# Two-layer transformer block, head size 8: the head outputs of a step issued ahead of its scores

## The chip, the cores and the metric

The kernel runs on one core of one Trainium2 chip. The metric is the time of one execution on the device in microseconds (us). Engines are named as the profile does: PE is TensorE (PEld its weight loads), ACT ScalarE, DVE VectorE, POOL GpSimd, SP SyncE.

## The reference

Sixty-four sequences of 128 tokens with width 160 go through two transformer layers. Each layer is self-attention, cross-attention over 77 context tokens of width 96, and a gated feed-forward part, each with a layer norm ahead of it and a residual behind it. The first layer has 20 heads of size 8, the second 20 heads of size 64. The part that matters here is the first layer's pair of attentions:

```python
def _attn(x, ctx, wq, wk, wv, wo, bo, heads):      # heads = 20, dh = 8
    q = (x @ wq).reshape(b, n, heads, dh).transpose(0, 2, 1, 3)
    k = (ctx @ wk).reshape(b, j, heads, dh).transpose(0, 2, 1, 3)
    v = (ctx @ wv).reshape(b, j, heads, dh).transpose(0, 2, 1, 3)
    sim = jnp.einsum('bhid,bhjd->bhij', q, k) * scale
    a = jax.nn.softmax(sim, axis=-1)
    out = jnp.einsum('bhij,bhjd->bhid', a, v)
    return out.transpose(0, 2, 1, 3).reshape(b, n, heads * dh) @ wo + bo
h1 = _ln(x, n1_g, n1_b)
x = _attn(h1, h1, q1, k1, v1, o1_w, o1_b, heads) + x
h2 = _ln(x, n2_g, n2_b)
x = _attn(h2, context, q2, k2, v2, o2_w, o2_b, heads) + x
```

## The kernel before

`attention_small` computes both attentions with head size 8. It takes four sequences at a time (a quad), 16 quads of self-attention and then 16 of cross-attention; the texts call these two halves the first and the second layer of this stage. A quad has ten units of work: five groups of four heads, each in two halves of two heads. So there are 320 units, numbered n, and as many steps k; the steps of a quad are its places s = k % 10. All loops are unrolled, and every engine has a hand-written order of its own, with semaphores between them.

Each unit goes through these hands:
1. `scores_step` (PE, line 890): eight products of two heads and four sequences into `scores`. Each uses 31 rows of the array, in two of its four row groups.
2. DVE takes the negated maximum over the keys (line 817) into `negmax`. At even places PE transposes the maxima of a finished group (line 1013), ACT copies them to `shift` (line 754), and a DMA that POOL issues (line 686) writes them as one more row of `q_stack`, so that the transposed scores come out with the maximum already subtracted.
3. `scoresT_step` (PE, line 908), five steps behind (`ST_LAG`): the transposed scores with that row, 32 rows of the array each, into `scoresT`. When its unit is k - 5 and the scores' unit is k, the two use different row groups.
4. ACT takes the exponential of the whole unit at once (line 731) into one of two `probs` buffers.
5. `values_step` (PE, line 927), six steps behind (`PV_LAG`): the head outputs, 16 records with 32 columns of the array each, into the single bank `heads_bank`. After the second half of a group ACT copies the bank to `heads` (line 761).

Both `scoresT` (its place) and `probs` tie these together. The transposed scores of unit n wait for the exponential of n - 1, the head outputs of unit n for the exponential of n; since the first is five steps and the second six steps behind, both wait in one step for the same exponential:

```python
# scoresT_step(k - 5)
if due(n):
    pe.wait_ge(s_exp, n)
...
# values_step(k - 6)
pe.wait_ge(s_exp, n + 1)
if half == 0 and due(n // 2):
    pe.wait_ge(s_heads, 5 * (k // QUNITS) + g)
```

Besides, a step of PE has other work, called the extras here: the projections for the next quad (places 0 to 3, line 332), norm transposes (4 and 6, line 428), the values' projections (8 and 9), the spreading of the reciprocal sums (1 and 3, line 1029), the output products (5 and 7, line 1087), and in the second layer fillers without use for the result (`keep_busy`, line 874).

ACT's order within a step is: the copy of a projected tile (line 720, places 1 to 4), the exponential (731), a copy of projected values (741, places 9 and 0), the norm's scaling (440, places 5 and 7), a rounding copy (450, places 6 and 8), the shift (754, even places), the copy of the head outputs (761, odd places). The exponential waits for this step's transposed scores, the copy at the end for this step's head outputs.

Ahead of this stage stand loads and constants, behind it the feed-forward part of the first layer and the second layer with its wide heads; these stages are the rest of the span.

Of the kernel before, what the change touches and what calls it, by code (L numbers as in the profile page):

```python
# [41 lines left out]
def live(value, total):  # L42

    return not isinstance(value, int) or 0 <= value < total


def due(count):

    return not isinstance(count, int) or count > 0
# [432 lines left out]
def attention_small(m, tag, wo, context, params, weights, state, front, following, following_params, first_gelu):  # L482
# [8 lines left out]
    ST_LAG, PV_LAG = 5, 6  # L491
# [6 lines left out]
    with ExitStack() as ctx:  # L498
# [89 lines left out]
        def maxima_at(k):  # L588

            s, local = k % QUNITS, k // QUNITS  # L590
            if s % 2:
                return None
            local, g = (local, s // 2 - 1) if s else (local - 1, GROUPS - 1)
            return (g, local % 2, 5 * local + g, local) if live(local, TOTAL) else None
# [267 lines left out]
        def _(pe):  # L862
# [14 lines left out]
            def scores_step(k):  # L877

                n, s, par, g, half = unit_of(k), k % QUNITS, k // QUNITS % 2, k % QUNITS // 2, k % 2
                if not live(n, LAST_UNIT):  # L880
                    return
                NK, EVEN = keys_of(quad_of(k)), even_of(quad_of(k))
                if due(n):
                    pe.wait_ge(s_negmax, n)
                if s < 2:
                    pe.wait_ge(s_stack[half], 16 * STACK_DMAS * (quad_of(k) + 1))
                for a in range(QUAD):
                    for jj in range(2):
                        rows = slice(32 * (2 * half + jj), 32 * (2 * half + jj) + 31)
                        last = nc.tensor.matmul(scores[:, jj, a * EVEN:(a + 1) * EVEN], q_stack[par][rows, g, a * P:(a + 1) * P],  # L890
                                                k_stack[par][rows, g, a * NK:a * NK + EVEN], start=True, stop=True)
                last.then_inc(s_scores, 1)

            def scoresT_step(k):

                n, par, g, half = unit_of(k), k // QUNITS % 2, k % QUNITS // 2, k % 2
                if not live(n, LAST_UNIT):
                    return
                NK = keys_of(quad_of(k))
                if due(n):  # L900
                    pe.wait_ge(s_exp, n)
                if half == 0:
                    order = 5 * (k // QUNITS) + g
                    pe.wait_ge(s_shift_in[order % 2], 16 * (order // 2 + 1))
                for a in range(QUAD):
                    for jj in range(2):
                        rows = slice(32 * (2 * half + jj), 32 * (2 * half + jj) + 32)
                        last = nc.tensor.matmul(scoresT[0:NK, jj, a * P:(a + 1) * P], k_stack[par][rows, g, a * NK:(a + 1) * NK],  # L908
                                                q_stack[par][rows, g, a * P:(a + 1) * P], start=True, stop=True)
                last.then_inc(s_scoresT, 1)  # L910

            def values_step(k):

                n, par, g, half = unit_of(k), k // QUNITS % 2, k % QUNITS // 2, k % 2
                if not live(n, LAST_UNIT):
                    return
                NK = keys_of(quad_of(k))
# [3 lines that stand above are left out]
                if k % QUNITS == 0:  # L921
                    pe.wait_ge(s_v, 2 * (quad_of(k) + 1))
                for r in range(2):
                    for b in range(2):
                        for jj in range(2):
                            c, a, col = 2 * b + jj, 2 * r + b, (2 * half + r) * P
                            last = nc.tensor.matmul(heads_bank[32 * c:32 * c + 32, col:col + P],  # L927
                                                    v[par][0:NK, a, GROUP * g + 2 * half + jj, :],
                                                    probs[k % 2][0:NK, jj, a * P:(a + 1) * P], start=True, stop=True)
                last.then_inc(s_pv, 1)  # L930
# [61 lines left out]
            def waiting(place):  # L992


                for i in range(START):
                    nc.tensor.matmul(place[:], wparts[0][0][0][:, 0:P], norm.high[0][:], start=True, stop=True)

            def step(k):
                s, local, ahead = k % QUNITS, k // QUNITS, quad_of(k) + 2
                if k == 0:  # L1000
                    waiting(max_bank)
                scores_step(k)
                scoresT_step(k - ST_LAG)
                values_step(k - PV_LAG)
                made = maxima_at(k)
                if made:
                    g, par, order, n = made
# [90 lines left out]
            def prepare(k):  # L1098
                if k == QUNITS - 1:
                    weights[0].wait_split(pe)  # L1100

            run(pe, step, prepare)


# [1258 lines left out]
```

## Time and profile before

| what | us |
|---|---|
| median of three runs | 3530.03 (3522.09 to 3530.37) |
| the profiled execution's own time | 3525.25 |
| its span, first to last instruction | 3522.1 |
| PE busy | 3457.5 (98% of the span) |
| DVE busy | 2319.1 (66%) |
| ACT busy | 2104.8 (60%) |
| POOL busy | 1290.1 (37%) |

PE is the busy engine over the whole span. The stage with head size 8 begins its steps near 35 us and its last one ends near 868 us. The granted clock is the share of full speed at which PE was allowed to run; 1.00 is 2.4 GHz, 0.50 is 1.2 GHz. Its mean over the span is 0.996.

### The profile page before, as it was taken

The numbers are of one execution on the slowest core, as the hardware profiler recorded it, in microseconds if no ns is written. First come the engines' busy times: TensorE is split into PE (matmuls) and PEld (weight loads), VectorE is DVE, ScalarE is ACT, GpSimd is POOL, SyncE is SP. The second block draws the span as 40 slices with busy tenths as digits, with TensorE's granted clock in tenths as the row PEclk, the third lists the DMA queues.
The fourth block names the chain that finished last, engine by engine and source line by source line (L and its number), as shares of the span: only waits on it lengthen the run. The fifth ranks groups of instructions, "written<-read, shape, count | busy, mean of one in ns | idle before, by whom it ended". The sixth has DMA issues, their size and how long they took to land. (4 is left out here: it accounts for less than half of the span.)

```text
span 3522.1 us, 96791 instructions
## 1 busy us (share of the span) xinstructions
PE 3457.5 (98%) x39199; PEld 3077.1 (87%) x39199; DVE 2319.1 (66%) x3902; ACT 2104.8 (60%) x5278; POOL 1290.1 (37%) x1278
## 2 busy tenths in 40 slices
PE   8999999999999999999999999899999999999999
PEld 6777778787888899999999999889999999998888
DVE  5788866665455567676776676656666666667454
ACT  4777777776334666566566556566666666665343
POOL 5333333332343243333333333433333333334332
PEclk9999999999999999999999999999999999999999
DMA  4444433321100100000000000000000000000000
GB/s 105 114 107 109 98 87 84 89 76 54 46 0 0 37 2 2 2 1 1 2 1 2 1 2 2 23 7 5 3 5 3 5 3 5 3 3 1 20 22 23
DMA packets 99756, 101.68 MB, mean 29 GB/s; under 512 B 31249, under 2 KB 74129, under 8 KB 99345
## 3 DMA queue, kind: packets, MB, share of 16 engines
q1 hardware_dynamic: 93408, 94.41, 10.6%
q8 instruction: 301, 4.93, 0.6%
q0 software_dynamic: 5120, 1.35, 0.2%
q14 instruction: 111, 0.90, 0.1%
q10 hardware_dynamic: 816, 0.08, 0.0%
HBM read 20.76 MB, written 5.24 MB: 7 GB/s over the span
## 5 line engine op out<-in xcount | busy, mean ns | idle before, releaser
L1217 POOL TENSOR_TENSOR a_probs<-a_probs,a_rsums 128x1024 f32<-128x1024 f32 x160 | 303.5, 1897 | 710.8 <-DVE a_rsums L1346 708.7
L1249 ACT ACTIVATE a_probs<-a_scores_banks,a_negmax 128x128 f32<-128x128 f32 x1280 | 371.4, 386 | 197.5 <-DVE a_negmax L1325 197.5
L1666 POOL TENSOR_TENSOR c_probs<-c_probs,c_rsums 128x616 f32<-128x616 f32 x160 | 233.9, 1462 | 618.1 <-DVE c_rsums L1795 618.1
L731 ACT ACTIVATE s_probs<-s_scoresT_banks 128x1024 f32<-128x1024 f32 (+1 forms) x320 | 327.1, 1022 | 182.7 <-PE s_scoresT_banks L908 180.4
L817 DVE TENSOR_REDUCE s_negmax<-s_scores_banks 128x8 f32<-128x1024 f32 (+1 forms) x320 | 322.2, 1007 | 134.3 <-PE s_scores_banks L890 130.9
L1703 ACT ACTIVATE c_probs<-c_scores_banks,c_negmax 128x77 f32<-128x77 f32 x1280 | 311.6, 334 | 133.9 <-DVE c_negmax L1783 133.1
L1354 DVE COPY a_probsT<-a_scores_banks 128x1024 f32<-128x1024 f32 x160 | 195.6, 1223 | 170.0 <-PE a_scores_banks L1422 169.9
L1783 DVE TENSOR_REDUCE c_negmax<-c_scores_banks 128x4 f32<-128x308 f32 x320 | 138.2, 473 | 238.8 <-PE c_scores_banks L1874 195.3
L2169 DVE SCALAR_TENSOR_TENSOR f_hidden<-f_value_bank,bias,f_gate 128x512 f32<-128x512 f32 x160 | 120.1, 750 | 246.8 <-ACT f_gate L2144 244.8
L686 POOL DMA_DIRECT2D s_q_stack<-s_shift x160 | 93.6, 585 | 488.9 <-ACT s_shift L754 482.5
L2144 ACT ACTIVATE f_gate<-f_gate_bank,bias 128x512 f32<-128x512 f32 x160 | 109.9, 687 | 260.9 <-PE f_value_bank L332 260.8
L1325 DVE TENSOR_REDUCE a_negmax<-a_scores_banks 128x4 f32<-128x512 f32 x320 | 198.6, 683 | 53.2 <-PE a_scores_banks L1409 53.2
L890 PEld LDWEIGHTS s_scores_banks<-s_k_stack,s_q_stack 31*128 31x128 f32 x2560 | 166.7, 185 | 72.5 <-issue 39.8
L1344 DVE TENSOR_REDUCE a_sums<-a_probs 128x8 f32<-128x1024 f32 x160 | 194.2, 1214 | 52.1 <-ACT a_probs L1249 52.1
L890 PE MATMUL s_scores_banks<-s_k_stack,s_q_stack 31*128 31x128 f32 (+1 forms) x2560 | 208.0, 283 | 6.0 <-DVE s_negmax L817 3.2
L927 PE MATMUL s_heads_bank<-s_probs,s_v 128*32 128x128 f32 (+1 forms) x5120 | 206.6, 279 | 0.7
L1714 ACT COPY c_queries<-c_even_bank 128x512 f32<-128x512 f32 x160 | 93.7, 586 | 189.6 <-PE c_even_bank L332 187.5
L2227 PEld LDWEIGHTS f_y_bank<-f_w_out,f_hidden 128*128 128x128 f32 x1280 | 190.9, 189 | 17.1 <-DVE f_hidden L2169 3.9
L1939 PE MATMUL c_y_bank<-w_out,c_outT 128*128 128x160 f32 x1280 | 203.0, 302 | 0.9 <-DVE c_outT L1774 0.9
L2227 PE MATMUL f_y_bank<-f_w_out,f_hidden 128*128 128x160 f32 x1280 | 200.5, 299 | 2.5 <-DVE f_hidden L2169 2.5
L1459 PE MATMUL a_y_bank<-w_out,a_outT 128*128 128x160 f32 x1280 | 199.6, 303 | 1.8 <-DVE x_tokens L1336 1.8
L1271 ACT COPY a_v<-a_even_bank 128x512 f32<-128x512 f32 (+1 forms) x192 | 96.0, 519 | 168.6 <-PE a_even_bank L332 99.0
(319 smaller groups left out, 10473.8 us busy)
## 6 DMA issues: line engine op xcount, KB each, us to landing
s_q_stack<-front SPq DMA_DIRECT2D x192, 160.0 KB, 3.3
s_k_stack<-front SPq DMA_DIRECT2D x96, 160.0 KB, 3.8
s_out<-s_heads SPq DMA_DIRECT2D x128, 80.0 KB, 2.5
s_k_stack<-front SPq DMA_DIRECT2D x96, 96.2 KB, 3.0
x_tokens<-in_x SPq DMA_DIRECT2D x16, 320.0 KB, 3.7
out_x<-x_tokens SPq DMA_DIRECT2D x16, 320.0 KB, 2.4
s_q_stack<-s_shift POOLq DMA_DIRECT2D x160, 8.0 KB, 2.5
s_ctx_in<-in_ctx SPq DMA_DIRECT2D x16, 115.5 KB
```

The source lines that it names most:

```text
L731: nc.scalar.activation(probs[i][0:NK, :, :], scoresT[0:NK, :, :], ACT.Exp).then_inc(s_exp, 1)
L817: nc.vector.tensor_reduce(out=negmax[order % 2][:, half * 2 * QUAD:(half + 1) * 2 * QUAD].rearrange("p (j a) -> p j a", j=2), in_=scores[: ...
L890: last = nc.tensor.matmul(scores[:, jj, a * EVEN:(a + 1) * EVEN], q_stack[par][rows, g, a * P:(a + 1) * P], k_stack[par][rows, g, a * NK:a ...
L927: last = nc.tensor.matmul(heads_bank[32 * c:32 * c + 32, col:col + P], v[par][0:NK, a, GROUP * g + 2 * half + jj, :], probs[k % 2][0:NK, j ...
L1217: nc.gpsimd.tensor_tensor(probs[n % 4][:], probs[n % 4][:], rsums[n % 2][:].unsqueeze(2).broadcast_to([P, UNIT, TOK]), ALU.mult).then_inc( ...
L1249: last_one = nc.scalar.activation(probs[n % 4][:, h, :], scores[n % 2][:, h // GROUP, h % GROUP * TOK:(h % GROUP + 1) * TOK], ACT.Exp, bia ...
L1325: nc.vector.tensor_reduce(out=negmax[n % 2][:, j * GROUP:(j + 1) * GROUP], in_=scores[n % 2][:, j, :].rearrange("p (h k) -> p h k", h=GROU ...
L1459: last = nc.tensor.matmul(y_bank[:, a * D:(a + 1) * D], outT[n % 2][:, (2 * c + a) * P:(2 * c + a + 1) * P], m.wo[:, 2 * g + c, :], start= ...
L1666: nc.gpsimd.tensor_tensor(probs[n % 5][:], probs[n % 5][:], rsums[n % 2][:].unsqueeze(2).broadcast_to([P, UNIT, NK]), ALU.mult).then_inc(s ...
L1703: last_one = nc.scalar.activation(probs[n % 5][:, h, :], scores[:, h // GROUP, h % GROUP * NK:(h % GROUP + 1) * NK], ACT.Exp, bias=negmax[ ...
L1939: last = nc.tensor.matmul(y_bank[:, a * D:(a + 1) * D], outT[n % 2][:, (2 * c + a) * P:(2 * c + a + 1) * P], m.wo[:, 2 * g + c, :], start= ...
L2227: last = nc.tensor.matmul(y_bank[a // 2][:, a % 2 * D:(a % 2 + 1) * D], hidden[(k - 1) % 2][:, a * P:(a + 1) * P], w_out[:, t, :], start=( ...
```

## The change

In each step of PE, the head outputs of unit k - 6 are issued first, then the scores of unit k and the transposed scores of unit k - 5. No instruction is added or removed, the semaphores and lags are the same, and the orders of the other engines are not touched.

```diff
@@ -999,9 +999,9 @@
                 s, local, ahead = k % QUNITS, k // QUNITS, quad_of(k) + 2
                 if k == 0:
                     waiting(max_bank)
+                values_step(k - PV_LAG)
                 scores_step(k)
                 scoresT_step(k - ST_LAG)
-                values_step(k - PV_LAG)
                 made = maxima_at(k)
                 if made:
                     g, par, order, n = made
```

## Rows read from the trace of the kernel before

**Rows 1.** Busy us (x instructions), engines PE, PEld, DVE, ACT, POOL; clock, DMA, GB/s.

```profile
35.00:868.00 833.00, 820.25 (x13190) 640.28 (x13190) 598.32 (x941) 610.72 (x976) 289.79 (x361) 1.00 0.37 93
```

**Rows 2.** Waits, 35 to 868 us: waiter, awaited, total us, times, longest.

```profile
PEld s_scores_banks L890 <- DVE s_negmax L817: 28.4, 76, 1.0
...
PEld s_scoresT_banks L908 <- ACT s_probs L731: 0.8, 2, 0.4
```

**Rows 3.** Timeline of PE, place 0, first layer: start, duration, instruction.

```profile
319.69 0.33 PE L890 MATMUL s_scores_banks<-s_k_stack,s_q_stack 31*128 31x128 f32 x2
319.72 0.33 PE L908 MATMUL s_scoresT_banks<-s_q_stack,s_k_stack 32*128 32x128 f32 x2
...
320.40 0.65 PE L927 MATMUL s_heads_bank<-s_probs,s_v 128*32 128x128 f32 x16
320.98 0.28 PE L1013 MATMUL s_max_bank<-ident,s_negmax 128*16 128x128 f32 x1
```

**Rows 4.** Timeline of ACT, places 2 to 1 of the first layer.

```profile
301.08 1.03 ACT L731 ACTIVATE s_probs<-s_scoresT_banks 128x1024 f32<-128x1024 f32 x1 [0.98 <-PE s_scoresT_banks L908]
...
303.40 1.03 ACT L731 ACTIVATE s_probs<-s_scoresT_banks 128x1024 f32<-128x1024 f32 x1
...
306.54 1.02 ACT L731 ACTIVATE s_probs<-s_scoresT_banks 128x1024 f32<-128x1024 f32 x1 [0.98 <-PE s_scoresT_banks L908]
...
308.55 1.02 ACT L731 ACTIVATE s_probs<-s_scoresT_banks 128x1024 f32<-128x1024 f32 x1 [0.85 <-PE s_scoresT_banks L908]
...
310.13 0.59 ACT L761 COPY s_heads<-s_heads_bank 128x512 f32<-128x512 f32 x1
311.10 1.02 ACT L731 ACTIVATE s_probs<-s_scoresT_banks 128x1024 f32<-128x1024 f32 x1 [0.38 <-PE s_scoresT_banks L908]
...
318.17 1.02 ACT L731 ACTIVATE s_probs<-s_scoresT_banks 128x1024 f32<-128x1024 f32 x1 [0.84 <-PE s_scoresT_banks L908]
...
319.60 0.66 ACT L761 COPY s_heads<-s_heads_bank 128x512 f32<-128x512 f32 x1
320.49 1.02 ACT L731 ACTIVATE s_probs<-s_scoresT_banks 128x1024 f32<-128x1024 f32 x1 [0.23 <-PE s_scoresT_banks L908]
...
322.90 1.02 ACT L731 ACTIVATE s_probs<-s_scoresT_banks 128x1024 f32<-128x1024 f32 x1
```

**Rows 5.** Timeline of ACT, places 2 to 0 of the second layer.

```profile
503.85 1.02 ACT L731 ACTIVATE s_probs<-s_scoresT_banks 77x1024 f32<-77x1024 f32 x1 [0.96 <-PE s_scoresT_banks L908]
...
505.92 1.02 ACT L731 ACTIVATE s_probs<-s_scoresT_banks 77x1024 f32<-77x1024 f32 x1 [0.25 <-PE s_scoresT_banks L908]
506.84 0.57 ACT L761 COPY s_heads<-s_heads_bank 128x512 f32<-128x512 f32 x1
...
508.51 1.02 ACT L731 ACTIVATE s_probs<-s_scoresT_banks 77x1024 f32<-77x1024 f32 x1 [0.79 <-PE s_scoresT_banks L908]
...
510.61 1.02 ACT L731 ACTIVATE s_probs<-s_scoresT_banks 77x1024 f32<-77x1024 f32 x1 [0.94 <-PE s_scoresT_banks L908]
...
512.19 0.57 ACT L761 COPY s_heads<-s_heads_bank 128x512 f32<-128x512 f32 x1
513.48 1.02 ACT L731 ACTIVATE s_probs<-s_scoresT_banks 77x1024 f32<-77x1024 f32 x1 [0.71 <-PE s_scoresT_banks L908]
...
520.88 1.02 ACT L731 ACTIVATE s_probs<-s_scoresT_banks 77x1024 f32<-77x1024 f32 x1 [0.75 <-PE s_scoresT_banks L908]
...
523.73 1.02 ACT L731 ACTIVATE s_probs<-s_scoresT_banks 77x1024 f32<-77x1024 f32 x1 [0.25 <-PE s_scoresT_banks L908]
```

**Rows 6.** Timeline of PE near 127 us; in brackets idle time, releaser.

```profile
126.85 0.66 PE L908 MATMUL s_scoresT_banks<-s_q_stack,s_k_stack 32*128 32x128 f32 x8 [0.72 <-DMA s_q_stack<-s_shift]
127.44 0.43 PE L927 MATMUL s_heads_bank<-s_probs,s_v 128*32 128x128 f32 x8
```

**Rows 7.** Timeline of PE near 96 us; in brackets idle time, releaser.

```profile
96.35 0.37 PE L1013 MATMUL s_max_bank<-ident,s_negmax 128*16 128x128 f32 x1 [1.82 <-DVE s_out L804]
```

**Rows 8.** Busy times and granted clock as in rows 1, 96.09 to 102.92.

```profile
96.09:102.92 6.83, 6.57 (x45) 4.27 (x46) 4.33 (x7) 3.44 (x7) 3.57 (x4) 0.50 0.01 1
```

## The prediction

> **What bounds the kernel now.** I first looked at the busy times of the stretch in which the changed loop runs. TensorE is busy for 820.25 of 833 us there, ScalarE for 610.72, VectorE for 598.32 [rows 1]. So one step of this loop costs what TensorE's own instructions cost, and anything that makes TensorE stand still is added to the time. The wait rows say how little it stands now: for VectorE's maxima before the scores 28.4 us in all, and for ScalarE's exponentials 0.8 us in two places [rows 2]. The reader should not conclude that the exponentials are far from being needed. The timeline has to tell how much earlier than needed each one ends.
>
> One step of TensorE [rows 3]: scores and transposed scores start together at 319.69 and 319.72 (they lie in different row groups and run side by side), the head outputs follow at 320.40, the rest of the step ("the extras": maxima, projections, norm transposes, output products, fillers) at 320.98. The exponential starts at 320.49 [rows 4], 0.80 us after the pair began. So it runs beside the head outputs and the extras, and the next step's pair is the first that needs it.
>
> **What the change does.** No instruction is added or removed; the 16 records of the head outputs change place, 313 times (units 6 to 318, counted over both layers; in the other steps one of the two partners is missing, which I cost at nothing, since the fillers and start-up waits there are longer). Head outputs of k-6 and transposed scores of k-5 need the same exponential, that of unit k-6. Before, the scores of k stand ahead of both. After, the head outputs stand at the very front.
>
> Two things follow. First, the exponential of a step starts later in the step, by the head outputs' length: 320.40 to 320.98 is 0.58 us [rows 3], and it must be over before the next step's first instruction. The work that hides it shrinks from head outputs plus extras to extras alone. Second, the bank of the head outputs is single. In every second step the head outputs also wait for ScalarE's copy out of it (line 761), which stands in ScalarE's order behind the exponential and behind whatever else the step has (the norm's line 440, the values' copy of line 741). Today the pair of scores covers that copy; then nothing does. Queued behind the waiting head outputs on TensorE are scores, transposed scores and extras, that is everything; ScalarE waits in turn for the transposed scores, VectorE for the scores. It closes into a ring.
>
> **The ring's length.** From one exponential's start to the next: exponential 1.02 us [rows 4], release of TensorE, head outputs 0.58, pair to next exponential 0.80 [rows 3]. The release is not seen for an exponential. The nearest row is the copy that ends at 319.60 + 0.66 = 320.26 [rows 4], after which the head outputs start at 320.40 [rows 3], while usually they follow the pair sooner: 0.14 us. That gives 1.02 + 0.14 + 0.58 + 0.80 = 2.54 us. Where a heads copy stands between, with its end h after the exponential's start, it is h + 1.52 us. A step takes the longer of this and today's interval between exponentials.
>
> First layer [rows 4], by place in the quad (ten steps):
> - place 2: 303.40 - 301.08 = 2.32, loses 0.22. Place 3: 3.14, and with the second layer's h of 1.49 [rows 5] the ring is 3.01: loses nothing; place 1 likewise.
> - place 4: 2.01, loses 0.53. Place 6 has the same form, 0.53.
> - place 5: 2.55; the norm's activation comes first and the copy ends at 310.72, h = 2.17, ring 3.69, loses 1.14. Place 7 has the same form, 1.14.
> - place 9: 2.32; h = 320.26 - 318.17 = 2.09, ring 3.61, loses 1.29.
> - place 0: 2.41, loses 0.13. Place 8 is left out (near 2.5).
> Sum 4.98 us a quad. 154 of the steps are here, 15.4 quads: 77 us.
>
> Second layer [rows 5], whose extras are longer by the fillers: place 2: 2.07, loses 0.47. Place 3: 2.59; h = 1.49, ring 3.01, loses 0.42. Place 4: 2.10, loses 0.44, place 6 the same. Place 5: 2.87; h = 2.15, ring 3.67, loses 0.80, place 7 the same. Place 9: 2.85; with the first layer's h of 2.09 the ring is 3.61, loses 0.76. Place 0 as in the first layer, 0.13. Sum 4.26 us, 159 steps, 15.9 quads: 68 us.
>
> Together 145 us. The profiled execution took 3525.25 us (span 3522.1 and 3.15 around it), so it would take 3670; the median of the three runs is 3530.03, 5 us above that, and the same 145 us on it give 3675.
>
> **What I cost at nothing.** Scores to maxima to scores: the same instructions lie between them in either order, and a ring of 2.54 us is longer than today's shortest interval of 2.01 us [rows 4]. So the 28.4 us [rows 2] may shrink a little; they lie inside the intervals already. The shift's DMA through GpSimd: shift copy and transposed scores both move back by 0.58 us. If its cover were gone it would show as a wait like the 0.72 us at 126.85 [rows 6]. SyncE's DMAs are issued in the same order at the same places; nothing is moved past them. The later stages begin after the loop and aren't touched.
>
> **The one unseen cost.** Head outputs directly followed by scores don't occur in the trace: from column groups to row groups of the array. Low end: the scores start right at the issue rate, after 0.65 - 0.28 = 0.37 us [rows 3] (16 records, the last of which ends 0.28 after its start, as the record of line 1013 does), 0.21 less. High end: the same 0.21 more. Nearest row: from head outputs to a full-array instruction, 0.58 us, which I take, because the step has three changes of form before and three after. Over 313 steps the ends are 66 us off on either side, 3609 and 3741 us. In a sentence that the sum can do without: TensorEngine Tiling (Array Packing), Key Properties, of the Trainium skill says that changing the tiling mode drains TensorE while going from one tile to another doesn't; by that rule this change of form costs as the others do and the sum stays 3675, while an unpriced change would give 3609. The trace agrees for the neighbouring case (0.58 us where 0.37 would do).
>
> **Rivals.**
> - *The clock falls.* The new waits are 1.29 us at place 9, and 1.14 at place 5 with 0.53 at place 6 behind it. The trace has one case: a wait of 1.82 us before 96.35 and then 6.83 us at a granted clock of 0.50 (1.2 GHz instead of 2.4) [rows 7, 8]. Against it: the longest new wait is shorter than that, and the clock was full through the 0.72 us one [rows 6]. At half clock, 6.83 us do at most 3.4 us less work. Once per quad in the first layer: 16 x 3.4 = 54 us more, 3729; in all 31 quads 105 us, 3780. In a sentence by itself: TensorE: Matmul & The Clock Gate, What's actually happening, of the Trainium skill says that activity is what keeps the full clock granted, by which more standing still is a risk.
> - *Only the exponential binds, the copies don't.* That is so if heads copies are already over. First layer 0.13 + 0.22 + 0.53 + 0.53 + 0.22 (place 9) = 1.63, second 0.13 + 0.47 + 0.44 + 0.44 = 1.48; 25 + 24 = 49 us, 3579. Against it: at 320.40 the head outputs are already held by such a copy although the pair is ahead of them.
> - *The cheap change of form*, 3609, as above; for it speaks only that it wasn't seen.
> - *Not slower: TensorE passes the waiting head outputs.* If its queue let the scores go ahead of head outputs whose exponential isn't there, the old order would come back by itself and the time stay 3530. It decides from the first blocked instruction. Against it: when the transposed scores waited for a DMA until 126.85, the head outputs behind them, which had their data, started at 127.44 only [rows 6].
>
> **Chances and range.** Forecast 0.66 (its own range: 7 of 10 places are bound in the first layer and 8 in the second, 108 + 127 = 235 steps, and a release of nothing to twice 0.14 us moves each by 0.14 us, together 33 us: 3642 to 3708), clock 0.13, cheap change 0.07, dear change 0.03, exponential alone 0.05, passing 0.03, and 0.03 for a gain by something I don't see. The range leaves out the last three cases (0.11) and the upper half of the clock's (0.07): 3605 to 3745. About 0.3% is what this measurement can tell from no change: slower 0.93, same 0.04, faster 0.03.
>
> **What would show it.** In the changed profile the wait of line 927 for ScalarE's lines 731 and 761 is some 145 us where it was nothing; the waits of ScalarE for the transposed scores grow by as much; TensorE's busy time is the same, in a loop of about 978 us; intervals between exponentials are 2.5 at even places, 3.6 to 3.7 at places 5, 7 and 9. Wrong it would be if line 927 waits only at even units' exponentials, if scores start less than 0.5 us after head outputs, or if the clock is below 1.00 in the loop.

## The result and the profile after

The changed kernel takes 3899.8 us (four runs, 3896.3 to 3903.6) where the kernel before takes 3529.3: a ratio of 1.105 (1.104 to 1.107), 370 us more. The forecast was 3675, with 3605 to 3745 as its range. The direction was right and the time far outside. What the forecast had called a rival of 0.13, a falling clock, is most of the loss, and a clock below 1.00 in the loop was among its own signs of being wrong.

The page of the profile after, with the lines that answer to the table of before (span; busy us, share and instructions; busy tenths and granted clock in 40 slices):

```profile
span 3893.5 us, 96791 instructions
PE 3757.6 (97%) x39199; PEld 3297.4 (85%) x39199; DVE 2307.4 (59%) x3902; ACT 2101.5 (54%) x5278; POOL 1290.8 (33%) x1278
...
PE   7888889999999998999999999999999999999999
...
PEclk9888896556566999999999999999999999999999
```

The same 39199 records of TensorE are busy for 300 us longer. A kernel that only waits more keeps its busy time; this one does the same work more slowly. The clock row says where: from the first slice to the 13th, that is in the loop with head size 8, and, to a tenth, nowhere behind it.

The same in two stretches and a part of the second, as in [rows 1] (busy us of PE, PEld, DVE, ACT, POOL, then the granted clock):

```profile
58.00:560.00 502.00, 437.22 (x6058) 326.52 (x6058) 309.66 (x442) 288.21 (x462) 139.80 (x175) 0.85 0.35 84
...
560.00:1240.00 680.00, 663.35 (x6909) 519.15 (x6907) 261.30 (x478) 309.59 (x499) 143.07 (x177) 0.60 0.18 48
668.83:859.98 191.15, 191.15 (x1778) 150.07 (x1771) 67.74 (x132) 80.89 (x132) 40.00 (x50) 0.50 0.17 46
```

Two different troubles can be read here. In the first layer TensorE stands still for 65 of 502 us and has a clock of 0.85. In the second it stands still for 17 of 680 us only, and its clock is 0.60. For 191 us on end (third line) it is at half clock, 1.2 GHz, and busy without a gap: TensorE waits for nothing, and every step takes longer.

What TensorE did before such a stretch differs too. In the first layer 14 of the 15 falls come within 2 us of a wait of 1.1 to 1.3 us of the head outputs for the heads copy (line 761). The second layer has five long stretches at half clock, from 590, 669, 884, 962 and 1133 us on, and each begins 0.4 to 1.8 us after the end of a wait of 0.76 or 0.77 us of another instruction, line 1095. The first two:

```profile
588.54 0.47 PE L1095 MATMUL s_even_bank<-ident,s_ctx_in 77*96 77x77 f32 x4 [0.76 <-ACT s_v L741]
...
668.13 0.47 PE L1095 MATMUL s_even_bank<-ident,s_ctx_in 77*96 77x77 f32 x4 [0.77 <-ACT s_v L741]
```

This instruction transposes the context for a quad to come. It isn't part of the ring, and the forecast doesn't have it; e3 below shows where its wait comes from.

Where the clock is full, the ring of the forecast is seen. TensorE's timeline at places 5 to 7 of a quad of the first layer (in brackets idle time and what ended it):

```profile
320.61 0.65 PE L927 MATMUL s_heads_bank<-s_probs,s_v 128*32 128x128 f32 x16 [0.54 <-ACT s_probs L731]
321.18 0.33 PE L890 MATMUL s_scores_banks<-s_k_stack,s_q_stack 31*128 31x128 f32 x2
...
321.80 1.35 PE L1087 MATMUL s_odd_bank<-s_w_out,s_out 80*128 80x160 f32 x8
324.24 0.65 PE L927 MATMUL s_heads_bank<-s_probs,s_v 128*32 128x128 f32 x16 [1.09 <-issue]
...
326.69 0.64 PE L927 MATMUL s_heads_bank<-s_probs,s_v 128*32 128x128 f32 x16 [0.54 <-ACT s_probs L731]
```

And ScalarE's beside it, places 4 to 6, which answers to [rows 4]:

```profile
319.53 1.02 ACT L731 ACTIVATE s_probs<-s_scoresT_banks 128x1024 f32<-128x1024 f32 x1 [1.17 <-PE s_scoresT_banks L908]
320.45 0.24 ACT L754 CAST s_shift<-s_max_bank 16x128 fp32r<-16x128 f32 x1
321.98 1.02 ACT L731 ACTIVATE s_probs<-s_scoresT_banks 128x1024 f32<-128x1024 f32 x1 [1.29 <-PE s_scoresT_banks L908]
322.90 0.77 ACT L440 ACTIVATE quad_y<-s_even_bank,norm_cols 128x512 f32<-128x512 f32 x1
323.56 0.59 ACT L761 COPY s_heads<-s_heads_bank 128x512 f32<-128x512 f32 x1
325.61 1.02 ACT L731 ACTIVATE s_probs<-s_scoresT_banks 128x1024 f32<-128x1024 f32 x1 [1.47 <-PE s_scoresT_banks L908]
```

From exponential to exponential it is 321.98 - 319.53 = 2.45 us at place 4 (forecast 2.54, before 2.01) and 325.61 - 321.98 = 3.63 at place 5 (forecast 3.69, before 2.55). The exponential ends at 320.55 and the head outputs start at 320.61: the release that I had no row for is 0.06 us, not 0.14. The heads copy of place 5 ends at 324.15 and the head outputs of place 6 start at 324.24, behind a wait of 1.09 us. The trace puts that wait down to "issue", not to the copy. I take it for the copy's, because the same step two places on has 1.14 us and names the copy (line 761). The scores start 321.18 - 320.61 = 0.57 us after the head outputs, so the change of form between them costs what I took (0.58).

### The profile page after: what moved, and what is told of

It reads as the page before. It is cut to its first block and busy times, and to the rows that moved or that the text cites. A ratio compares the mean times of both kernels' runs of the same rounds, so it can differ in the third digit from the quotient of the medians.

```text
span 3893.5 us, 96791 instructions
## 1 busy us (share of the span) xinstructions
PE 3757.6 (97%) x39199; PEld 3297.4 (85%) x39199; DVE 2307.4 (59%) x3902; ACT 2101.5 (54%) x5278; POOL 1290.8 (33%) x1278
## 5 line engine op out<-in xcount | busy, mean ns | idle before, releaser
L927 PE MATMUL s_heads_bank<-s_probs,s_v 128*32 128x128 f32 (+1 forms) x5120 | 273.6, 346 | 75.8 <-ACT s_heads L761 34.6
L890 PEld LDWEIGHTS s_scores_banks<-s_k_stack,s_q_stack 31*128 31x128 f32 x2560 | 227.9, 248 | 94.5 <-issue 93.6
L927 PEld LDWEIGHTS s_heads_bank<-s_probs,s_v 128*32 128x32 f32 (+1 forms) x5120 | 155.9, 132 | 176.9 <-issue 108.3
L890 PE MATMUL s_scores_banks<-s_k_stack,s_q_stack 31*128 31x128 f32 (+1 forms) x2560 | 274.0, 346 | 1.3 <-DMA s_k_stack<-front 1.1
L908 PE MATMUL s_scoresT_banks<-s_q_stack,s_k_stack 32*128 32x128 f32 (+1 forms) x2560 | 233.8, 314 | 0.0
L2227 PEld LDWEIGHTS f_y_bank<-f_w_out,f_hidden 128*128 128x128 f32 x1280 | 190.9, 189 | 17.1 <-DVE f_hidden L2169 3.9
```

The costliest lines, as they stand in the source:

```text
L2227: last = nc.tensor.matmul(y_bank[a // 2][:, a % 2 * D:(a % 2 + 1) * D], hidden[(k - 1) % 2][:, a * P:(a + 1) * P], w_out[:, t, :], start=( ...
```

## The experiments

Each time stands beside runs of the kernel before on the same chip. They are medians of four runs (after), two (e1, e2, e3, e9), eight (e8), eleven (b3) and twelve (b1); e4, e5, e6 and e10 ran once, so that only their large differences count. The last three columns come from one trace of each: the time from the first exponential to the 156th (the first layer), from there to the last (the second), and the granted clock's mean over the whole span.

| kernel | us | before | first layer | second layer | clock |
|---|---|---|---|---|---|
| before | 3529.3 | | 397.2 | 419.2 | 0.996 |
| after | 3899.8 | 3529.3 | 511.3 | 678.2 | 0.909 |
| e1: fillers in the waits | 3658.9 | 3527.3 | 468.4 | 483.9 | 0.993 |
| e2: heads copy first | 3674.6 | 3527.3 | 427.2 | 560.9 | 0.952 |
| e3: and lag 7 | 3782.8 | 3527.3 | 404.5 | 667.3 | 0.922 |
| e6: before without fillers | 3658.1 | 3527.3 | 396.5 | 549.5 | 0.941 |
| e4: order in the first layer only | 3651.4 | 3526.9 | 519.3 | 420.5 | 0.971 |
| e5: order in the second only | 3762.5 | 3526.9 | 400.0 | 653.8 | 0.933 |
| e8: e3 and values' copy first | 3527.7 | 3526.9 | 400.6 | 419.3 | 0.997 |
| e9: e2 and values' copy first | 3561.0 | 3526.9 | 409.8 | 435.1 | 0.996 |
| e10: bursts in every quad | 3832.2 | 3526.4 | 518.2 | 605.9 | 0.936 |
| b3: e8 and the norm's stack first | 3524.2 | 3526.4 | 393.5 | 422.5 | 0.994 |
| b1: before, values' copy first | 3519.3 | 3526.4 | 395.2 | 413.7 | 0.995 |

The first question was whether the clock costs anything by itself, since at half clock TensorE might only fill the time that it would otherwise wait.

**e1_fill**

```diff
-    KEEP = {2: 3, 4: 3, 5: 4, 6: 3, 7: 4, 8: 6, 9: 4}
+    KEEP = {2: 5, 3: 2, 4: 5, 5: 9, 6: 5, 7: 9, 8: 6, 9: 8}
+    KEEP_FIRST = {4: 3, 5: 8, 6: 3, 7: 8, 9: 9}
...
                 count = extra if crossed(n) and n < TOTAL else early
+                if 2 <= n < QUADS:
+                    count = KEEP_FIRST.get(s, 0)
```

> The changed kernel with more fillers (products of unused result, 0.11 us each) put into the extras of the steps in which TensorE now stands still: in the first layer 3, 8, 3, 8 and 9 at places 4, 5, 6, 7 and 9, in the second 2, 2, 2, 5, 2, 5 and 4 more at places 2 to 7 and 9. They take about as long as the waits they replace. Theory (the ring of waits costs about 120 us and the rest of the 370 us is TensorE's granted clock): the clock stays at 1.00 in the loop and the time is near 3650, between 3630 and 3670, faster than the changed kernel although it does more work. Rival (the waits alone are the loss, the half clock only fills time that the ring would have wasted): the time stays near 3900.

Measured: 3658.9 us, ratio 1.037 (1.034 to 1.040). The changed kernel gains 241 us by being given more to do. By the table 43 us of that come in the first layer and 194 in the second. Its second layer, to be read against the second line of the changed kernel's two stretches:

```profile
518.00:1003.00 485.00, 470.24 (x7238) 378.37 (x7240) 270.88 (x478) 306.04 (x499) 142.61 (x177) 0.99 0.26 68
```

More records (7238 against 6909), less busy time (470 against 663 us), clock 0.99. So the 370 us are 132 us of ring at nearly full clock (3658.9 - 3527.3, where the forecast had 145) and 241 us of clock (3899.8 - 3658.9; each beside its own runs of before, 2 us apart). A little of the 132 is clock too: e1 has 34 us at half clock in the loop, before has 7, which is at most 14 us of lost work. The forecast's sum with the measured release of 0.06 instead of 0.14 us would be 10 us smaller, 135: it applies to the steps bound by the exponential, four places of a quad, 125 steps. The fillers at place 9 also cut the wait of line 1095 to 0.32 us, so e1 doesn't tell this wait from those of the ring.

Next, the ring's two branches, taken apart.

**e2_copy_first**

The copy of line 761 moves up, ahead of the exponential (line 731):

```diff
+                n, kk = unit_of(k - PV_LAG), k - PV_LAG
+                if kk % 2 == 1 and live(n, LAST_UNIT):
...
+                    nc.scalar.copy(heads[kk // QUNITS % 2][:, g, :], heads_bank[:]).then_inc(s_heads, 1)
                 n = unit_of(k - ST_LAG)
                 if live(n, LAST_UNIT):
...
-                n, kk = unit_of(k - PV_LAG), k - PV_LAG
-                if kk % 2 == 1 and live(n, LAST_UNIT):
...
-                    nc.scalar.copy(heads[kk // QUNITS % 2][:, g, :], heads_bank[:]).then_inc(s_heads, 1)
```

> The changed kernel with ScalarE's copy of the head outputs issued ahead of the step's exponential instead of last in the step. Theory (two branches of the ring, the copy's being the longer one at places 3, 5, 7 and 9): intervals at places 5, 7 and 9 fall from 3.6 us to today's TensorE work (2.5 in the first layer, 2.9 in the second), only the exponential's branch of 2.44 us is left, about 37 us over the loop at full clock; the clock falls in few places or in none, so 3565 to 3620. Rival (the exponential is the whole ring): no change, near 3900. Rival (half clock in the second layer holds itself up whatever the waits): 3700 to 3800.

**e3_lag7**: the same and

```diff
-    ST_LAG, PV_LAG = 5, 6
+    ST_LAG, PV_LAG = 5, 7
```

> As e2_copy_first, and the head outputs lag the scores by seven steps instead of six, so that at the front of a step they need an exponential that ended a step ago. Theory: the ring is opened, nothing waits at the front of a step, the order of issue itself costs nothing: 3515 to 3545, clock 1.00. Rival (head outputs followed by scores is a dear change of form of the array, or the order disturbs something else): 3560 or more.

**e6_no_fill**

```diff
-    KEEP = {2: 3, 4: 3, 5: 4, 6: 3, 7: 4, 8: 6, 9: 4}
+    KEEP = {}
```

> The kernel before with the second layer's fillers left out (line 492 empty; the bursts stay), no other change. Theory (the second layer holds its full clock only by a small margin): TensorE's own work falls by some 50 us, yet the clock falls in the second layer of this stage and the time rises, 3560 to 3700. Rival (the clock doesn't hang on them): 3480 to 3530.

e2 did to the intervals what was expected: at full clock 2.48 us at places 5 and 7 of the first layer and 2.87 in the second, where the changed kernel has 3.63 and 3.60. At place 9 of the second layer the interval stayed at 3.43 us, which the expectation didn't have. Its time was missed: 3674.6 (two runs, 3649.8 and 3699.4), since in its trace, that of the longer run, the second layer was at half clock for some 290 of 561 us. e3 was missed by 240 us. Its first layer was as hoped (404.5 us), yet its second took 667, as if nothing had been mended. The trace of e3 shows why. TensorE at place 9 of quad 21, and then three stretches with their clock:

```profile
617.96 0.24 PE L332 MATMUL s_odd_bank<-s_w_high,s_ctx_low 96*77 96x160 f32 x1
618.96 0.47 PE L1095 MATMUL s_even_bank<-ident,s_ctx_in 77*96 77x77 f32 x4 [0.76 <-ACT s_v L748]
619.36 1.08 PE L927 MATMUL s_heads_bank<-s_probs,s_v 77*32 77x128 f32 x16
```

```profile
598.91:619.39 20.48, 19.72 (x346) 16.35 (x346) 13.19 (x18) 14.64 (x23) 6.05 (x8) 1.00 0.36 97
619.39:674.00 54.61, 54.61 (x504) 42.02 (x503) 19.84 (x43) 24.59 (x39) 11.66 (x15) 0.50 0.16 43
674.00:694.48 20.48, 19.73 (x342) 16.34 (x341) 13.11 (x18) 14.64 (x23) 6.16 (x8) 1.00 0.38 99
```

One wait of 0.76 us, and 0.4 us behind it the head outputs take 1.08 us instead of 0.65. Then 54.61 us at half clock, with TensorE busy in all of them, then 20.48 us at full clock, and the next fall, again behind a wait of 0.76 us of line 1095. All six falls in e3's loop from 452 us on stand directly behind a wait of line 1095 (0.75 to 1.12 us), and they last 55 to 147 us. In e2's trace both long stretches begin so too (0.76 and 0.77 us). The wait doesn't bring a fall each time, though: seven of e2's, from 808 us on, passed at full clock. The waiting instruction transposes the context into a bank that ScalarE's copy of the values (line 741 in the kernel before) must have read. That copy stands behind the exponential, and the new order starts the exponential 0.58 us later in a step. In the kernel before, the same wait was 0.19 us in 14 of 15 quads. That is a third branch which the forecast hadn't seen: it weighed line 741 only for the heads copy behind it, not for who waits for line 741 itself.

e6 shows the same fragility in the old order: the kernel before without its fillers has less work and takes 3658.1 us; its second layer's clock averages 0.64. The fillers were cover as well as work: without them the wait of line 1095 is 0.64 us instead of 0.19. One of e6's two long stretches (92 us) begins beside such a wait, the other (297 us) doesn't, so a lack of work and a longer wait aren't told apart in it.

**e4_first_layer** and **e5_second_layer** divide the change. The diff is that of e4; e5 has k >= QUADS * QUNITS in both places:

```diff
+                if k < QUADS * QUNITS:
+                    values_step(k - PV_LAG)
                 scores_step(k)
                 scoresT_step(k - ST_LAG)
-                values_step(k - PV_LAG)
+                if not k < QUADS * QUNITS:
+                    values_step(k - PV_LAG)
```

> The new order in the steps of the first layer only (k below 160), the old one in the second. Theory: the first layer loses what it lost in the changed kernel, 114 us, and the second, whose waits are the old ones, runs at full clock in 407 us: 3640, unless a low clock is carried over the border. Rival (the second layer loses its clock because the first has lost it): 3750 or more.

> The new order in the steps of the second layer only. Theory: the first layer takes its old 395 us, the second loses its clock by itself and takes 600 to 670 us instead of 407, so 3720 to 3790; together with e4_first_layer the two losses make up the 370 us. Rival (the first layer's falls are needed): second layer near 470 us, 3590.

Measured 3651.4 and 3762.5, that is 124 and 236 us over before, together 360 of the 370. The second layer loses its clock without help from the first (in e5 six falls, each behind a wait of line 1095's transposes of 0.76 or 0.77 us). And it does not lose it when its order is the old one, though it is entered at half clock: in e4 it takes 420.5 us.

**e8_lag7_values** and **e9_both_copies** test the reading of e3:

the copy of line 741 moves up too, ahead of the heads copy and the exponential:

```diff
+                values = values_at(k - 1)
+                if values:
+                    c, n, par = values
+                    act.wait_ge(s_vproj, 2 * n + c + 1)
...
                 n, kk = unit_of(k - PV_LAG), k - PV_LAG
                 if kk % 2 == 1 and live(n, LAST_UNIT):
...
```

> As e3_lag7, and ScalarE's copy of the projected values (places 9 and 0) is issued ahead of the exponential too, so that the context transposes at place 9 no longer wait 0.76 us for it. Theory (in e3 those waits alone let the clock fall, each fall stood directly behind one, and the second layer doesn't get it back by itself): the clock stays at 1.00 and the time is 3515 to 3545. Rival (the order itself, head outputs ahead of scores, keeps the second layer at half clock): near 3780 again.

> As e2_copy_first (lag six), with the values' copy ahead of the exponential too. Theory: the exponential's branch alone is left and the wait at place 9 is gone: 37 us over the loop, clock at 1.00, so 3560 to 3575. Rival (the exponential's waits of 0.3 to 0.45 us are enough to lose the clock in the second layer): 3640 or more.

e8 takes 3527.7 us, ratio 0.999 (0.996 to 1.002): no difference from before, with the head outputs ahead of the scores in every step, a lag of seven and two of ScalarE's copies moved. Moving one copy of ScalarE took 255 us off e3. The rows of line 1095 have no wait any more, where e3 had 14.0 us in 23 cases, and the second layer's clock is 1.00:

```profile
L1095 PE MATMUL s_even_bank<-ident,s_ctx_in x64: 227/229/235, 422.8 to 805.7; 77*96 77x77 f32 x64
its engine sat idle before it (us, times) until:
who waited for it (us, times):
```

```profile
450.00:869.00 419.00, 416.21 (x6888) 333.68 (x6889) 271.56 (x478) 312.89 (x498) 142.41 (x177) 1.00 0.30 79
```

e9, the same with the lag of six, keeps the exponential's branch alone: 3561.0 us, ratio 1.011 (1.007 to 1.015), 34 us. The waits for the exponential (line 749 there) that are left don't cost the clock:

```profile
PEld s_heads_bank L927 <- ACT s_probs L749: 92.7, 215, 1.3
...
PE s_heads_bank L927 <- ACT s_probs L749: 33.6, 92, 0.9
```

**e10_bursts**

```diff
-    BURST, BURST_QUADS = 12, (18, 23, 28)
+    BURST, BURST_QUADS = 12, tuple(range(16, 32))
```

> The changed kernel with the burst of 12 fillers at place 1 (until now in quads 18, 23 and 28) in every quad of the second layer, 13 more bursts of 1.3 us of work. Theory: the waits make the clock fall once a quad and a burst brings it back, so the half clock lasts for the last places of each quad only; the second layer takes 530 to 580 us instead of 661 and the kernel 3760 to 3815, although it has more work. Rival (the long half-clock stretches end by something else): 3900 to 3920.

3832.2 us and 605.9 us in the second layer: the right direction, but the gain was smaller than expected. In 11 of 16 quads places 2 to 7 now ran at full clock (5 in the changed kernel). Ten bursts met a half clock. In five of these quads it was full again by place 2; in the other five a burst of 12 did not bring it back, and place 1 took 8.21 us at half clock. Nor did the clock fall once a quad, as the theory had it: it fell five times, four of them directly behind a wait of 0.76 us of line 1095. What decides whether a burst succeeds stays open. The traces show only the place: in the changed kernel, e2, e3, e5, e6 and e10 every stretch of over 50 us that ended before quad 31 was done ended at place 1, the second of the two steps with projections of 512 columns (line 332), in quads with a burst and in quads without.

Two last kernels looked for a better version. **b3_lag7_stack** moves line 460 ahead of the maxima in VectorE's step, on top of e8; **b1_before_vfirst** is the kernel before with the values' copy ahead of the exponential, the edit of e8 and e9 alone.

> As e8_lag7_values, and VectorE's last part of the norm at place 9 (line 460) issued ahead of the step's maxima, since the scores now come 0.58 us later in a step and the projection at place 0 waited for that part. Theory: place 0 falls from 2.73 to about 2.4 us in the first layer and from 2.48 to 2.3 in the second, 8 us in all: 3515 to 3524 where e8 had 3527, ratio to before 0.997. Rival (the interval at place 0 is set by something else): no change against e8.

> The kernel before (old order, lag six) with ScalarE's copy of the projected values ahead of the exponential. Theory: the context transposes at place 9 wait 0.19 us (and up to 0.5) for it in 16 quads and no longer do, nothing else changes: 3 to 6 us less, ratio 0.998 to 1.000. Rival (the copy now delays the exponential, which the next pair needs): slower by 2 to 10 us.

b3: the interval at place 0 fell from 2.73 to 2.33 us and from 2.48 to 2.16, as expected, yet the time is 3524.2, ratio 0.999 (0.998 to 1.001), not to be told from before. In its trace the clock was at half for 17.1 us from 846.7 us on, beside a wait of 1.56 us, which takes back up to 9 us. b1: 3519.3, ratio 0.998 (0.997 to 0.999), 7 us less than before, little more than can be measured. No instruction of the context transposes waits in it.

## Why the prediction was wrong

- **What bounds the kernel.** Right: TensorE's own work, and everything that stops it adds up.
- **The ring.** Right as a mechanism. At full clock it costs 132 us (e1) where the sum had 145. The term that was too large is the release after an exponential, 0.06 us measured against 0.14 taken; 0.08 us in the places which the exponential binds. The copy's release is 0.15 (330.22 to 330.37) as taken, in some places 0.09 (324.15 to 324.24).
- **Its branches.** With the exponential alone the ring costs 34 us (e9; the rival's price was 49), so the copies make most of the other 98 of e1's 132; up to 14 of those are clock. ScalarE's order is what makes them bind: e2 moved one copy and the intervals at places 5 and 7 fell to TensorE's own work (2.87 us in the second layer) or to the exponential's branch (2.48 in the first). The scores behind the waiting head outputs at 324.24 stood still with them, which ends the rival of passing. TensorE: Matmul & The Clock Gate, Architectural detail, of the Trainium skill has ScalarE's queue as strictly first in, first out, so that only the order of issue can help; the trace agrees, since the copy at 323.56 started behind the norm's activation although the head outputs that it reads had ended at 321.26.
- **The change of form costs what the others do.** Right: 0.57 us. The order itself is nearly free, not quite: e8 equals before, but b1, the old order with the same values' copy moved, is 7 us below before, and e8 isn't. Place 0 takes 2.73 us in e8 and 2.33 in b1, and b3 brings it back to 2.33.
- **The clock, the step that failed.** The forecast gave this rival 0.13 and priced it at 6.83 us of half clock once per quad, 54 to 105 us, from the one fall before [rows 7, 8]. Both the chance and the price were wrong, and the wait that mattered most was not in the forecast. The argument against it ("the longest new wait is shorter" than 1.82 us) fails since the clock fell behind a wait of 0.76 us in e3, in a stretch that was busy for 19.72 of 20.48 us, and behind the same wait in the changed kernel. That wait, of the context transposes (line 1095) for the values' copy (line 741), stands before all five long falls of the changed kernel's second layer; among the forecast's waits it is missing. Removing it (e3 to e8, e2 to e9) gave the clock back. And the length isn't that of the one fall seen: in the changed kernel half clock lasts 3.4 to 20.5 us a time in the first layer and 55 to 191 us in the second. The price is 241 us, more than twice my upper end of 105.
- **What I should have read.** The fillers of line 492 stood in the second layer of the code, and e6 shows that without them it loses its clock. A loop in that state may have no room for new waits; this one had room for e9's and not for 0.76 us at place 9. The forecast treated these fillers as cover for the exponential only.
- **Chances.** Only 0.13 stood on the clock, and the range cut off the upper half of even that. Slower at 0.93 was right.

TensorE: Matmul & The Clock Gate, What's actually happening, of the Trainium skill, which the forecast cited for the risk, says that the gate follows how busy the engine has been. The pair e3 and e8 agrees for the fall, in that the clock stayed when a wait went. For the way back the rows show that being busy wasn't enough: 54.61 busy us of 54.61 at half clock in e3, 191.15 of 191.15 in the changed kernel.

## What to carry to other kernels

Before moving work to the front of an in-order step, list every event which that work waits for and every result that now comes later, and then everyone who waits for those: here the exponential, the bank's copy and, two engines on, the values' copy. A wait that the profile shows as 0.8 us in total says nothing about the margin; measure from the end of the awaited instruction to the first instruction that needs it. And where a kernel carries fillers for TensorE's clock, price any new wait by the clock it may lose: a run with fillers put into the new waits separates the two costs at once.

## What the runs showed of the hardware

- The clock's fall can cost far more than the wait behind which it comes: 0.75 or 0.76 us of waiting in e3's second layer were followed by 55 to 102 us at half clock, and 0.77 us in the changed kernel by 191. A quad takes some 45 us there and 25 in the kernel before. The same wait passed without a fall seven times in e2.
- TensorE at half clock and busy without a gap can stay there: 191 us in the changed kernel. Its first layer's falls were over after 20.5 us at most (44 us in e4; 48 in e2, across the border). What makes the two layers differ in this was not tried by itself and stays open.
- TensorE started 0.09 to 0.15 us after the end of ScalarE's copy that it waited for, and 0.06 us after the end of an exponential.
